# Expert sums in two half arrays, one bank for token and channel groups, and plain copies for five tiles

## The chip, the cores and the metric

The kernel runs on one core of a Trainium2 chip. The metric is the device time of one launch in microseconds; lower is better. PE is TensorE, DVE is VectorE, ACT is ScalarE, POOL is GpSimd, SP is SyncE with its DMA queue.

## The reference

The input x is (16, 64, 36, 100): batch, channel, height, width. The reference computes

```
y = x + sweeps(layernorm_over_channels(x))      # 9-tap convolutions with relu, row after row down and up, then column after column right and left
t = y as tokens (16*3600 tokens of 64 channels)
t = t + ffn(layernorm(t))
ffn(z): p = softmax(z @ router_w + router_b); the two largest of 8, rescaled to sum 1;
        sum over those two experts of p_e * (z @ expert_w[e] + expert_b[e])
```

The change touches only the last part, from the tokens on.

## The kernel before, in words

All of y stays in SBUF (`act_buf`), two image rows side by side: partitions 0 to 63 hold the channels of one row of a pair, partitions 64 to 127 those of the other. After the sweeps the token stage goes over the 18 row pairs. One row pair has 1600 columns (width times batch) in 13 tiles of 128, the last of which overlaps its neighbour and adds only 64 new columns (`TAIL`). The work of one row pair is called a region. Each region computes the experts of row pair j and, between them, prepares the tokens of row pair j + 1 (`now`). The last region prepares nothing. Buffers alternate by `slot`.

Preparation goes in 5 groups of up to three tiles (`TC`, `NCK`):

- `tokens` (PE, L974): y times a centring matrix with the router's columns behind it, 128 tokens by 144 columns, in PSUM bank `CT`, in two fp32 passes per tile.
- `copy_tokens` (ACT, L473 and L474): squares, and a copy to SBUF (`tl`).
- `square_sums` (DVE, L724), `inv_std_tokens` (ACT, L481 and L483): the inverse deviation.
- `scale_tokens` (POOL, L335 and L336): tokens and logits times the inverse deviation.
- `channels` (PE, L988): transposes back to channels, in bank `TB`.
- `first_part` (ACT, L491) and `second_part` (DVE, L732): high and low part of the normalised tokens, in fp32r.
- `softmax` (DVE, L748 to L764): 17 small steps for the whole row pair, with one exponential on ACT (L496), which give the gates of the two best experts and zero for the others.

The experts of a tile p:

- `experts` (PE, L1007): for each of the two image rows (q = 0, 1), 64 rows of the array, 512 columns (8 experts times 64 channels), three fp32r terms; q = 0 in the upper half of the array, q = 1 in the lower. The result is in one of two pairs of banks, `twin[0]` and `twin[1]`.
- `gate_tile` (DVE, L792): times the gates, into an SBUF buffer (`scratch`, `late` or `more`) of 8 experts by 128 columns. For tiles in `ACT_TILES` (6 to 12) DVE does only q = 0 and `gate_odd` (ACT, L506) does q = 1 with 8 instructions, one per expert, since the gate is then one scalar per partition.
- `pair_sums` (POOL, L322): experts 0 to 3 plus experts 4 to 7, 512 elements in place.
- `sum_experts` (PE, L1019): four full 128 x 128 transposes that accumulate in bank `SUM`, `LAG` = 2 tiles behind the experts. A gathering of four tiles (`QUAD`) fills the bank.
- `add_out` (DVE, L800): the bank plus y, into y.

SP stores a row pair when all its additions are done.

The order of each engine's instructions is written out by hand: a loop over the 13 tiles, with tables and fixed offsets that say beside which tile each piece of preparation stands. `STEP_AT` places the softmax steps. Engines meet through semaphores: `s_p` experts done, `s_g` and `s_ga` gated by DVE and ACT, `s_ps` pair sum done, `s_y` sum done, `s_o` addition done, `s_cp` token group copied, `s_xn2` group scaled, `s_tb`, `s_th` and `s_tl` channel group, its high part and its low part done. `experts` of tile p waits for the gating of tile p - 2. The first sum of a gathering waits for the addition of the gathering before.

```
for p in range(TILES):                    # the region on PE, before
    experts(j, slot, p)
    if now is not None:
        if 5 <= p < NCK + 5: channels(now, 1 - slot, p - 5)
        if p < NCK: tokens(now, 1 - slot, p)
    if p >= LAG: sum_experts(j, slot, p - LAG)
    elif later(j): sum_experts(j - 1, 1 - slot, TILES + p - LAG)
```

Of the kernel before, what the change touches and what calls it, by code (L numbers as in the profile page):

```python
# [7 lines left out]
ALU = mybir.AluOpType  # L8
# [4 lines left out]
def metaformer_kernel(nc, x, x_col, w_d, w_u, w_r, w_l, router_w, router_b, expert_w, expert_b, out):  # L13
# [24 lines left out]
    with ctx:  # L38
# [40 lines left out]
        gated = [scratch[:, 0:E * P], scratch[:, E * P:2 * E * P], late[:, 0:E * P], more[:, :]]  # L79
        gated = [g.rearrange("p (e m) -> p e m", e=E) for g in gated]  # L80
# [5 lines left out]
        sq = sb("sq", [P, 2, NC])  # L86
        lnv = sb("lnv", [P, 2, NC])
        rstd = sb("rstd", [P, 2, NC])
# [33 lines left out]
        def act_gates(j, p):  # L122

            return len(ACT_TILES) * j + sum(a <= p for a in ACT_TILES)
# [12 lines left out]
        def stage_age(slot, p):  # L137

            k = TILES * slot + p
            return next(d for d in range(1, SEQ) if stage_of(k - d) == stage_of(k))  # L140
# [5 lines left out]
        def later(n):  # L146
# [8 lines left out]
        STEP_AT = [(6, 2), (7, 0), (7, 1), (7, 2), (8, 0), (8, 1), (8, 2), (9, 0), (9, 2), (10, 0), (10, 1), (10, 2),  # L155
                   (11, 0), (11, 1), (11, 2), (12, 0), (12, 1)]
        EXP_TILE = STEP_AT[GAP_STEP - 1][0] + 1

# [106 lines left out]
        def _(pool):  # L265
# [51 lines left out]
            def pair_sums(j, slot, p):  # L317
                pool.wait_ge(s_g, TILES * j + p + 1)
                if p in ACT_TILES:
# [18 lines left out]
            def region(j, slot, now):  # L338
                for p in range(TILES):
                    if now is not None and 2 <= p < NCK + 2:  # L340
                        scale_tokens(now, 1 - slot, p - 2)
                    pair_sums(j, slot, p)
# [12 lines left out]
        def _(act):  # L355
# [109 lines left out]
            def copy_tokens(j, slot, c, bank=CT):  # L465
# [19 lines left out]
            def first_part(j, slot, c, bank=TB):  # L485
# [24 lines left out]
            def region(j, slot, now):  # L510

                for p in range(TILES):
                    if now is not None:
                        if p == EXP_TILE:
                            exponential(now)
                        if 5 <= p < NCK + 5:
                            first_part(now, 1 - slot, p - 5)
                        if p < NCK:
                            copy_tokens(now, 1 - slot, p)
                    if p in ACT_TILES:  # L520
                        gate_odd(j, slot, p)
                    if now is not None and 1 <= p < NCK + 1:
                        inv_std_tokens(now, 1 - slot, p - 1)
# [18 lines left out]
        def _(dve):  # L542
# [184 lines left out]
            def second_part(j, slot, c, bank=TB):  # L727
# [39 lines left out]
            def softmax(j, slot, at):  # L767

                steps = softmax_steps(j, slot)
                for k in range(SMN):  # L770
                    if STEP_AT[k] == at:
                        if k == 0:
                            dve.wait_ge(s_xn2, NCK * (j + 1))
                        elif k == EX_STEP:
                            dve.wait_ge(s_ex, j + 1)
                        if k > 0:
                            dve.wait_ge(s_sm, SMN * j + k)
                        steps[k]().then_inc(s_sm, 1)

            def gate_tile(j, slot, p):  # L780
# [7 lines left out]
                qs = 1 if p in ACT_TILES else 2  # L788
# [5 lines left out]
            def add_out(j, g):  # L794

                lo, hi = g * QUAD, min((g + 1) * QUAD, TILES)
                width, off = (QUAD * TN, 0) if hi < TILES else (TAIL, TN - TAIL)
                dst = flat(j)[:, lo * TN:lo * TN + width]
                dve.wait_ge(s_y, TILES * j + hi)
                nc.vector.tensor_tensor(dst, banks[SUM][:, off:off + width], dst, ALU.add).then_inc(s_o, 1)  # L800
# [10 lines left out]
            def region(j, slot, now):  # L811

                for p in range(TILES):
                    if now is not None and 1 <= p < NCK + 1:
                        square_sums(now, 1 - slot, p - 1)
                    gate_tile(j, slot, p)
                    if now is not None and 5 <= p < NCK + 5:
                        second_part(now, 1 - slot, p - 5)
                    for part in range(3):
                        if part == 2:  # L820
                            add_behind(j, p)
                        if now is not None:
                            softmax(now, 1 - slot, (p, part))
# [6 lines left out]
            for p in range(TILES):  # L830
                for part in range(3):
                    softmax(0, 0, (p, part))
# [12 lines left out]
        def _(pe):  # L845
# [120 lines left out]
            def tokens(j, slot, c, bank=CT):  # L966
# [11 lines left out]
            def channels(j, slot, c, bank=TB):  # L978
# [3 lines left out]
                if bank == TB:  # L982
                    if later(n):
                        pe.wait_ge(s_tl, n)
                elif c >= 2:
                    pe.wait_ge(s_tl, n - 1)
# [5 lines left out]
            def experts(j, slot, p):  # L992
# [6 lines left out]
                if p >= 2:  # L999
                    if p - 2 in ACT_TILES:  # L1000
                        pe.wait_ge(s_ga, act_gates(j, p - 2))
                elif later(j) and TILES + p - 2 in ACT_TILES:
# [8 lines left out]
            def sum_experts(j, slot, p):  # L1011
# [5 lines left out]
                at = (p % QUAD) * TN  # L1017
                for e in range(E // 2):
                    last = mm(banks[SUM][:, at:at + TN], stage(slot, p)[:, e], ident[:, :],  # L1019
                              start=e == 0, stop=e == E // 2 - 1, is_transpose=True)  # L1020
                last.then_inc(s_y, 1)

            def region(j, slot, now):
                for p in range(TILES):
                    experts(j, slot, p)
                    if now is not None:
                        if 5 <= p < NCK + 5:
                            channels(now, 1 - slot, p - 5)
                        if p < NCK:
                            tokens(now, 1 - slot, p)  # L1030
                    if p >= LAG:
                        sum_experts(j, slot, p - LAG)
                    elif later(j):
                        sum_experts(j - 1, 1 - slot, TILES + p - LAG)

# [82 lines left out]
```

## Time and profile before

| | |
|---|---|
| median of 3 runs | 1408.58 us (1408.44 to 1409.0) |
| the profiled execution's own time | 1407.74 us |
| span of the profiled execution | 1406.0 us |
| token stage: first gating, last addition begins | 936.51 us, 1401.78 us |
| one region with preparation | 25.97 us |

The span is the time between the first and the last recorded instruction of one execution; the rest of the run's time lies around it. Page shares are of the whole span. In the rows below, a group of instructions is named by its line in the kernel. A matmul's record is longer than its share of the array, since successive ones overlap. Durations of groups (xN) run from the first start to the last end.

### The profile page before, as it was taken

How to read it: one execution, taken by the hardware profiler on the slowest of the kernel's cores; microseconds unless marked ns; L12 is line 12 of the kernel's file. 1: busy time of each engine (PE TensorE's matmuls, PEld its weight loads, DVE VectorE, ACT ScalarE, POOL GpSimd, SP SyncE). 2: the span in 40 equal slices, each digit the busy share in tenths (PEclk: the TensorE clock that was granted, in tenths of full speed). 3: DMA queues.
4: the chain of work that ended last, by engine and by line, in shares of the span. 5: the costliest groups of instructions: out<-in, count | busy, mean ns of one | idle time of the engine just before them, and what ended most of it. 6: DMA issues, size and time to landing. Idle time of an engine off the chain costs nothing.

```text
span 1406.0 us, 30169 instructions
## 1 busy us (share of the span) xinstructions
PE 1345.1 (96%) x9344; PEld 1180.1 (84%) x9344; DVE 854.8 (61%) x1786; ACT 670.4 (48%) x2169; POOL 625.9 (45%) x752
## 2 busy tenths in 40 slices
PE   6899999999998999999999999979999999999997
PEld 5899999999998999999999999956666666666664
DVE  4788888755555222222222222269989989889896
ACT  5576777533434222222100000048778778778775
POOL 3566666100000000000144444457787887887886
PEclk9999999999999999999999999989999999999999
DMA  4112121100000000000011111100010100100101
GB/s 146 48 47 70 47 70 47 43 0 0 0 0 0 0 0 0 0 0 0 21 63 63 63 63 63 42 1 25 30 42 24 47 25 24 48 24 24 48 24 48
DMA packets 15372, 46.68 MB, mean 33 GB/s; under 512 B 2912, under 2 KB 2912, under 8 KB 15328
## 3 DMA queue, kind: packets, MB, share of 16 engines
q1 hardware_dynamic: 15184, 45.76, 9.3%
q8 instruction: 28, 0.46, 0.1%
q10 hardware_dynamic: 144, 0.33, 0.1%
q14 instruction: 16, 0.13, 0.0%
HBM read 31.33 MB, written 14.75 MB: 33 GB/s over the span
## 4 chain that ended last, share of the span: by engine, by line
PE 85%; DVE 6%; ACT 4%; issue 3%; POOL 1%; DMA 0%; DVEq 0%; POOLq 0%; ACTq 0%
PE twin L951 33%; PE twin L868 26%; PE twin L1007 9%; PE twin L1019 6%; PE twin L974 5%; PE twin L859 2%; PE twin L853 2%; PE twin L988 2%; ACT late L506 1%; DVE parts L732 1%; DVE scratch L792 1%; ACT more L506 1%; DVE act_buf L800 1%; ACT parts L491 1%; DVE twin L750 0%
## 5 line engine op out<-in xcount | busy, mean ns | idle before, releaser
L951 PE MATMUL twin<-kbuf,late 128*128 128x136 f32 (+2 forms) x3940 | 458.2, 280 | 5.0 <-DVE kbuf L700 5.0
L951 PEld LDWEIGHTS twin<-kbuf,late 128*128 128x128 f32 x3940 | 458.0, 192 | 5.3 <-DVE kbuf L700 5.3
L868 PE MATMUL twin<-parts 128*128 128x384 f32 (+2 forms) x2070 | 392.8, 341 | 0.0
L868 PEld LDWEIGHTS twin<-parts 128*128 128x128 f32 x2070 | 371.2, 188 | 2.8 <-issue 2.5
L297 POOL TENSOR_TENSOR act_buf<-kbuf,x_in 128x144 f32 (+1 forms) x198 | 96.6, 488 | 564.8 <-DVE kbuf L706 564.8
L706 DVE SCALAR_TENSOR_TENSOR kbuf<-twin,act_buf 128x144 f32<-128x144 f32 x394 | 121.3, 308 | 337.2 <-PE twin L951 337.2
L1007 PE MATMUL twin<-em,parts 64*128 64x512 f32 x1404 | 227.7, 429 | 5.0 <-DVE scratch L792 2.7
L322 POOL TENSOR_TENSOR scratch<-scratch 128x512 f32<-128x512 f32 x126 | 160.7, 1278 | 53.7 <-ACT scratch L506 36.7
L473 ACT ACTIVATE x_in<-twin 128x384 f32<-128x384 f32 (+1 forms) x90 | 40.3, 447 | 302.0 <-PE twin L974 302.0
L1007 PEld LDWEIGHTS twin<-em,parts 64*128 64x128 f32 x1404 | 116.7, 186 | 55.0 <-issue 36.7
L459 ACT ACTIVATE act_buf<-kbuf 128x144 f32 x196 | 63.2, 323 | 167.5 <-DVE kbuf L706 167.5
L792 DVE TENSOR_TENSOR scratch<-twin,scratch 128x512 f32<-128x512 f32 (+1 forms) x126 | 120.1, 953 | 17.3 <-PE twin L1007 13.1
L506 ACT ACTIVATE scratch<-twin,scratch 128x64 f32<-128x64 f32 x504 | 113.5, 415 | 0.8 <-PE twin L1007 0.4
L279 POOL TENSOR_TENSOR x_parts<-x_in,eps_c 128x400 fp32r<-128x400 f32 x66 | 56.3, 853 | 99.2 <-PE twin L853 81.0
L1019 PE MATMUL twin<-ident,scratch 128*128 128x128 f32 x504 | 78.4, 278 | 19.3 <-DVE act_buf L800 16.5
L281 POOL TENSOR_TENSOR x_parts<-x_in,x_parts 128x400 fp32r<-128x400 f32 x66 | 92.8, 1407 | 5.2
L322 POOL TENSOR_TENSOR late<-late 128x512 f32<-128x512 f32 x63 | 80.6, 1280 | 26.1 <-ACT late L506 19.0
L974 PEld LDWEIGHTS twin<-cl_w,act_buf 128*128 128x128 f32 x468 | 63.2, 193 | 34.2 <-ACT x_in L474 24.8
L1019 PEld LDWEIGHTS twin<-ident,scratch 128*128 128x128 f32 x504 | 56.4, 141 | 39.6 <-POOL scratch L322 34.3
L431 ACT ACTIVATE parts<-scratch 128x400 fp32r<-128x400 f32 x68 | 36.6, 538 | 106.7 <-DVE scratch L656 106.7
L974 PE MATMUL twin<-cl_w,act_buf 128*128 128x144 f32 x468 | 81.9, 309 | 2.1 <-POOL act_buf L314 2.0
L577 DVE TENSOR_TENSOR act_buf<-twin,rstd 64x400 f32 (+1 forms) x132 | 75.3, 570 | 1.9
(102 smaller groups left out, 1535.8 us busy)
## 6 DMA issues: line engine op xcount, KB each, us to landing
x_in<-x SPq DMA_DIRECT2D x36, 400.0 KB, 3.5
x_in<-x_col SPq DMA_DIRECT2D x20, 720.0 KB, 4.1
result<-act_buf SPq DMA_DIRECT2D x36, 400.0 KB, 2.8
scratch<-L_conv_w_d ACTq DMA_DIRECT2D x1, 320.0 KB, 4.7
scratch<-L_conv_w_u SPq DMA_DIRECT2D x1, 320.0 KB, 6.1
late<-L_conv_w_r SPq DMA_DIRECT2D x1, 320.0 KB, 6.4
late<-L_conv_w_l SPq DMA_DIRECT2D x1, 320.0 KB, 7.2
ew<-L_ffn_expert_w SPq DMA_DIRECT2D x2, 128.0 KB, 6.2
```

The lines of the kernel that those rows point to most:

```text
L281: nc.gpsimd.tensor_tensor(x_parts[:, b, 1], src, x_parts[:, b, 0].bitcast(F32), ALU.subtract).then_inc(s_xp, 1)
L297: nc.gpsimd.tensor_tensor(cols[:, :, g, w], kbuf[:, g], x_blk[:, slot, i, g], ALU.add).then_inc(s_cb[g], 1)
L322: nc.gpsimd.tensor_tensor(buf[:, 0:4], buf[:, 0:4], buf[:, 4:8], ALU.add).then_inc(s_ps, 1)
L506: last = act.activation(stage(slot, p)[:, e, C:P], twin[(TILES * slot + p) % 2][:, 1, e * C:(e + 1) * C], ACT.Copy, scale=gate[slot][:, 2 ...
L577: return nc.vector.tensor_tensor(rows[a * C:(a + 1) * C, 2 * j + q, g], centred[half], inv[half], ALU.mult)
L706: nc.vector.scalar_tensor_tensor(kbuf[:, g], banks[CONV[g]][:, 0:NH].rearrange("p (j b) -> p j b", j=HP), 0.0, cols[:, :, g, w], ALU.max, ...
L792: nc.vector.tensor_tensor(dst, src, scl, ALU.mult).then_inc(s_g, 1)
L868: last = mm(acc[:, lo:hi], vw[:, k, wpart, si], carry[:, cpart, g, lo + s * BG:hi + s * BG], start=first and si == 0, stop=final and si == ...
L951: last = mm(banks[CONV[g]][:, lo * BG:hi * BG], hw[:, k, si], kbuf[:, g, lo + s:hi + s].rearrange("p j b -> p (j b)"), start=si == 0, stop ...
L974: last = mm(banks[bank][:, CLW * i:CLW * (i + 1)], flat[:, tile_lo(p):tile_lo(p) + TN], cl_w[:, :], start=True, stop=True)
L1007: last = mm(twin[(TILES * slot + p) % 2][:, q, 0:E * C], tok[half, slot, l, span], em[half, b], start=k == 0, stop=k == len(TERMS) - 1)
L1019: last = mm(banks[SUM][:, at:at + TN], stage(slot, p)[:, e], ident[:, :], start=e == 0, stop=e == E // 2 - 1, is_transpose=True)
```

## The change

- Expert sums: each transpose is done as two half-array transposes, tokens 0 to 63 and 64 to 127 of the tile, each from its own 64 partitions, with 64 columns of the identity, into two banks (`SUMS`, 4 and 5). A bank holds 64 columns for each of eight tiles, so `QUAD` is 8, and two gatherings per region (8 and 5 tiles) take the place of four. An addition reads both banks in one instruction; the last gathering has one for four tiles and one for the tail.
- Token and channel groups share one bank (`CTB`, 7), so each group waits for the one before to be read out.
- `ACT_TILES` becomes (9, 11, 12). For `COPY_TILES` (0, 6, 7, 8, 10) ACT copies the q = 1 half without gates in one instruction of 512 elements, POOL multiplies that half by the gates in place of its addition, and PE sums all 8 experts instead of 4. Tile 0 is thus no longer gated whole by DVE.
- `LAG` is 3. There are six gated buffers instead of four; the two new ones lie on `sq`, `lnv` and `rstd`, which the token stage doesn't use. A buffer comes round after five tiles in most cases.
- Tables place every piece of the preparation. At one place PE does channels before tokens, ACT does the exponential, high parts, deviations, then copies, and DVE reductions, low parts, then softmax steps.

```diff
-        CT, TB = 4, 5
-        LOG, SUM = 6, 7
+        SUMS, LOG, CTB = [4, 5], 6, 7
-        FILL_CT, FILL_TB = [4, 0, 1, 2, 3], [5, 7, 5, 7, 5]
-        ACT_TILES = (6, 7, 8, 9, 10, 11, 12)
+        FILL_CT, FILL_TB = [7, 0, 1, 2, 3], [4, 5, 7, 4, 5]
+        ACT_TILES = (9, 11, 12)
+        COPY_TILES = (0, 6, 7, 8, 10)
-        LAG = 2
+        LAG = 3
-        QUAD = 4
+        QUAD = 8
-            return k % 4 if k < SEQ - 6 else (k - (SEQ - 6)) % 3
+            return k if k < 6 else (k - 6) % 5
-        STEP_AT = [(6, 2), (7, 0), (7, 1), (7, 2), (8, 0), (8, 1), (8, 2), (9, 0), (9, 2), (10, 0), (10, 1), (10, 2),
-                   (11, 0), (11, 1), (11, 2), (12, 0), (12, 1)]
+        TURN_AT = [(0, 0), (1, 1), (2, 1), (3, 1), (4, 1)]
+        COPY_AT = [(0, 0), (1, 0), (2, 1), (3, 1), (4, 1)]
+        VAR_AT = [(0, 0), (2, 0), (3, 0), (3, 2), (4, 2)]
+        INV_AT = [(2, 1), (3, 1), (4, 0), (5, 1), (6, 0)]
+        SCALE_AT = [(2, 0), (3, 0), (4, 0), (4, 0), (4, 0)]
+        BACK_AT = [(5, 1), (7, 0), (7, 1), (9, 0), (11, 0)]
+        HIGH_AT = [(6, 0), (6, 1), (8, 0), (8, 1), (10, 1)]
+        LOW_AT = [(5, 2), (7, 0), (7, 2), (9, 0), (11, 0)]
+        STEP_AT = [(6, 2), (7, 1), (7, 1), (8, 0), (8, 0), (8, 1), (9, 0), (10, 0), (10, 2), (11, 0), (11, 0), (11, 1), (11, 1), (12, 0), (12, 1), (12, 1), (12, 2)]
+        EXP_AT = (10, 1)
...
 pair_sums (POOL):
+                if p in COPY_TILES:
+                    odd = buf[:, :, C:P]
+                    scl = gate[slot][:, 2 * p + 1].unsqueeze(2).to_broadcast([P, E, C])
+                    nc.gpsimd.tensor_tensor(odd, odd, scl, ALU.mult).then_inc(s_ps, 1)
+                    return
                 nc.gpsimd.tensor_tensor(buf[:, 0:4], buf[:, 0:4], buf[:, 4:8], ALU.add).then_inc(s_ps, 1)
...
 gate_odd (ACT):
+                if p in COPY_TILES:
+                    src = twin[(TILES * slot + p) % 2][:, 1, :].rearrange("p (e c) -> p e c", e=E)
+                    act.activation(stage(slot, p)[:, :, C:P], src, ACT.Copy).then_inc(s_ga, 1)
+                    return
...
 add_out (DVE):
-                nc.vector.tensor_tensor(dst, banks[SUM][:, off:off + width], dst, ALU.add).then_inc(s_o, 1)
+                if hi < TILES:
+                    dst = flat(j)[:, lo * TN:hi * TN].rearrange("p (t r n) -> p r t n", r=2, n=C)
+                    src = twin[SUMS[0] // 2][:, :, 0:(hi - lo) * C].rearrange("p r (t n) -> p r t n", n=C)
+                    nc.vector.tensor_tensor(dst, src, dst, ALU.add).then_inc(s_o, 1)
...
 tokens (PE):
-                    if bank == CT:
+                    if c > 0 and bank == CTB:
                         pe.wait_ge(s_cp, n)
+                    elif c == 0:
+                        pe.wait_ge(s_tl, n)
...
 channels (PE), in a region:
+                elif c == 0:
+                    pe.wait_ge(s_cp, NCK * (j + 1))
+                else:
+                    pe.wait_ge(s_tl, n)
...
 sum_experts (PE):
-                at = (p % QUAD) * TN
-                for e in range(E // 2):
-                    last = mm(banks[SUM][:, at:at + TN], stage(slot, p)[:, e], ident[:, :],
-                              start=e == 0, stop=e == E // 2 - 1, is_transpose=True)
+                col, count = (p % QUAD) * C, E if p in COPY_TILES else E // 2
+                for e in range(count):
+                    for r in range(2):
+                        half = slice(r * C, (r + 1) * C)
+                        last = mm(banks[SUMS[r]][:, col:col + C], stage(slot, p)[half, e], ident[half, half],
+                                  start=e == 0, stop=e == count - 1, is_transpose=True)
                 last.then_inc(s_y, 1)
...
 the region on PE:
                 for p in range(TILES):
+                    for place in range(3):
+                        if place == 1:
+                            experts(j, slot, p)
+                        elif place == 2:
+                            if p >= LAG:
+                                sum_experts(j, slot, p - LAG)
+                            elif later(j):
+                                sum_experts(j - 1, 1 - slot, TILES + p - LAG)
+                        if now is not None:
+                            for c in at(BACK_AT, p, place):
+                                channels(now, 1 - slot, c)
+                            for c in at(TURN_AT, p, place):
+                                tokens(now, 1 - slot, c)
```

## Rows read from the trace of the kernel before

**Rows 1.** The page: busy us, share of the span and instructions of each engine.
```profile
PE 1345.1 (96%) x9344; PEld 1180.1 (84%) x9344; DVE 854.8 (61%) x1786; ACT 670.4 (48%) x2169; POOL 625.9 (45%) x752
```
**Rows 2.** Busy time by stretch, one region with preparation.
```profile
core 0: us, PE busy (x) PEld busy (x) DVE busy (x) ACT busy (x) POOL busy (x), PEclk, DMA share, GB/s
1113.25:1139.23 25.98, 24.61 (x169) 16.73 (x170) 23.42 (x45) 19.70 (x85) 21.00 (x24) 1.00 0.08 32
```
**Rows 3.** Timeline, PE: start, us, engine, line, operation, operands, count.
```profile
1110.48 0.30 PE L988 MATMUL twin<-ident,x_in 128*128 128x128 f32 x1 [0.16 <-DVE parts L732]
...
1113.25 0.63 PE L1019 MATMUL twin<-ident,scratch 128*128 128x128 f32 x4 [0.92 <-DVE act_buf L800]
1113.81 0.97 PE L1007 MATMUL twin<-em,parts 64*128 64x512 f32 x6
1114.70 0.66 PE L1019 MATMUL twin<-ident,scratch 128*128 128x128 f32 x4
1115.29 0.97 PE L1007 MATMUL twin<-em,parts 64*128 64x512 f32 x6
...
1119.93 1.00 PE L974 MATMUL twin<-cl_w,act_buf 128*128 128x144 f32 x6
...
1126.71 0.51 PE L974 MATMUL twin<-cl_w,act_buf 128*128 128x144 f32 x2
```
**Rows 4.** Timeline, PE, narrow window: two pairs of expert matmuls.
```profile
1113.81 0.73 PE L1007 MATMUL twin<-em,parts 64*128 64x512 f32 x4
```
**Rows 5.** Timeline, weight loads, narrow windows: two transpose loads, four expert loads.
```profile
1106.49 0.14 PEld L988 LDWEIGHTS twin<-ident,x_in 128*128 128x128 f32 x1 [0.37 <-POOL x_in L336]
...
1106.49 0.20 PEld L988 LDWEIGHTS twin<-ident,x_in 128*128 128x128 f32 x2 [0.37 <-POOL x_in L336]
...
1105.60 0.30 PEld L1007 LDWEIGHTS twin<-em,parts 64*128 64x128 f32 x4 [0.17 <-DVE late L792]
```
**Rows 6.** Timeline, DVE, in one region.
```profile
1110.65 0.37 DVE L753 TENSOR_TENSOR scratch<-rank_w,twin 128x208 f32<-128x208 f32 x1
1111.05 0.38 DVE L754 SCALAR_TENSOR_TENSOR twin<-scratch,twin 128x208 f32<-128x208 f32 x1
1111.34 0.68 DVE L792 TENSOR_TENSOR scratch<-twin,scratch 128x512 f32<-128x512 f32 x1
...
1118.14 1.23 DVE L792 TENSOR_TENSOR scratch<-twin,scratch 128x1024 f32<-128x1024 f32 x1 [0.30 <-DVE scratch L764]
1119.28 0.68 DVE L800 TENSOR_TENSOR act_buf<-twin,act_buf 128x512 f32 x1
1119.88 0.54 DVE L724 TENSOR_REDUCE stat<-x_in 128x6 f32<-128x384 f32 x1
1120.34 1.21 DVE L792 TENSOR_TENSOR late<-twin,scratch 128x1024 f32<-128x1024 f32 x1
```
**Rows 7.** Timeline, ACT, in one region.
```profile
1109.40 1.81 ACT L506 ACTIVATE scratch<-twin,scratch 128x64 f32<-128x64 f32 x8
1110.97 0.41 ACT L491 ACTIVATE parts<-twin 128x128 fp32r<-128x128 f32 x1
...
1118.86 0.49 ACT L473 ACTIVATE x_in<-twin 128x384 f32<-128x384 f32 x1 [0.67 <-PE twin L974]
```
**Rows 8.** Timeline, POOL, in one region.
```profile
1118.27 2.51 POOL L322 TENSOR_TENSOR scratch<-scratch 128x512 f32<-128x512 f32 x2 [0.35 <-ACT scratch L506]
...
1125.33 0.84 POOL L336 TENSOR_TENSOR x_in<-x_in,stat 128x384 f32<-128x384 f32 x1
...
1132.01 0.41 POOL L336 TENSOR_TENSOR x_in<-x_in,stat 128x128 f32<-128x128 f32 x1
```
**Rows 9.** PE's waits in one region: us in total, times, longest.
```profile
PE twin L1019 <- DVE act_buf L800: 0.9, 1, 0.9
```
**Rows 10.** Timeline, DVE: first gating and last addition of the last region.
```profile
1378.02 1.23 DVE L792 TENSOR_TENSOR scratch<-twin,scratch 128x1024 f32<-128x1024 f32 x1
...
1401.78 0.23 DVE L800 TENSOR_TENSOR act_buf<-twin,act_buf 128x64 f32<-128x64 f32 x1 [0.94 <-PE twin L1019]
```

More of the change, by code:

```diff
@@ L78, in metaformer_kernel @@
         sq_parts = parts[:, 2 * 2 * TOKS - 2 * 2 * NC:].rearrange("p (b l n) -> p b l n", b=2, l=2)
-        gated = [scratch[:, 0:E * P], scratch[:, E * P:2 * E * P], late[:, 0:E * P], more[:, :]]
-        gated = [g.rearrange("p (e m) -> p e m", e=E) for g in gated]
         early = act_buf[:, (HP - 8) * REG:(HP - 8) * REG + 3 * 4 * NC].rearrange("p (k b n) -> p k b n", k=3, b=4)
         kbuf = sb("kbuf", [P, G, HP, BG])
-        sq = sb("sq", [P, 2, NC])
-        lnv = sb("lnv", [P, 2, NC])
-        rstd = sb("rstd", [P, 2, NC])
+        spare = sb("spare", [P, 3 * 2 * NC])
+        sq, lnv, rstd = (spare[:, 2 * NC * k:2 * NC * (k + 1)].rearrange("p (b n) -> p b n", b=2) for k in range(3))
+        gated = [scratch[:, 0:E * P], scratch[:, E * P:2 * E * P], late[:, 0:E * P], more[:, :],
+                 spare[:, 0:E * P], spare[:, E * P:2 * E * P]]
+        gated = [g.rearrange("p (e m) -> p e m", e=E) for g in gated]
         ident = sb("ident", [P, P])
@@ L139, in stage_age @@
             k = TILES * slot + p
-            return next(d for d in range(1, SEQ) if stage_of(k - d) == stage_of(k))
+            return next(d for d in range(1, SEQ + 1) if stage_of(k - d) == stage_of(k))
         def tiles_of(c):
@@ L153, in metaformer_kernel, with at @@
         EX_STEP = 12
-        STEP_AT = [(6, 2), (7, 0), (7, 1), (7, 2), (8, 0), (8, 1), (8, 2), (9, 0), (9, 2), (10, 0), (10, 1), (10, 2),
-                   (11, 0), (11, 1), (11, 2), (12, 0), (12, 1)]
-        EXP_TILE = STEP_AT[GAP_STEP - 1][0] + 1
+        TURN_AT = [(0, 0), (1, 1), (2, 1), (3, 1), (4, 1)]
[8 more added lines that the diff above has]
+        EXP_AT = (10, 1)
+        def at(table, p, place):
+            return [c for c, when in enumerate(table) if when == (p, place)]
         s_wd = sem("s_wd")
@@ L339, in region @@
                 for p in range(TILES):
-                    if now is not None and 2 <= p < NCK + 2:
-                        scale_tokens(now, 1 - slot, p - 2)
-                    pair_sums(j, slot, p)
+                    for place in range(2):
+                        if place == 1:
+                            pair_sums(j, slot, p)
+                        if now is not None:
+                            for c in at(SCALE_AT, p, place):
+                                scale_tokens(now, 1 - slot, c)
             for c in range(NCK):
@@ L462, in _, with copy_tokens @@
                 copy_back(u, u)
-            def copy_tokens(j, slot, c, bank=CT):
+            def copy_tokens(j, slot, c, bank=CTB):
                 n, b, k = NCK * j + c, (slot + c) % 2, len(tiles_of(c))
@@ L512, in region @@
                 for p in range(TILES):
[L513 to L523, printed above, removed]
+                    for place in range(2):
+                        if place == 1 and p in ACT_TILES + COPY_TILES:
+                            gate_odd(j, slot, p)
+                        if now is not None:
+                            if EXP_AT == (p, place):
+                                exponential(now)
+                            for c in at(HIGH_AT, p, place):
+                                first_part(now, 1 - slot, c)
+                            for c in at(INV_AT, p, place):
+                                inv_std_tokens(now, 1 - slot, c)
+                            for c in at(COPY_AT, p, place):
+                                copy_tokens(now, 1 - slot, c)
             for c in range(NCK + 2):
@@ L765, in softmax_steps, with softmax @@
                 ]
[L767 to L778, printed above, removed]
+            def softmax(j, slot, k):
+                if k == 0:
+                    dve.wait_ge(s_xn2, NCK * (j + 1))
+                elif k == EX_STEP:
+                    dve.wait_ge(s_ex, j + 1)
+                if k > 0:
+                    dve.wait_ge(s_sm, SMN * j + k)
+                softmax_steps(j, slot)[k]().then_inc(s_sm, 1)
             def gate_tile(j, slot, p):
@@ L813, in region @@
                 for p in range(TILES):
[L814 to L820, printed above, removed]
+                    for place in range(3):
+                        if place == 1:
+                            gate_tile(j, slot, p)
+                        elif place == 2:
                             add_behind(j, p)
                         if now is not None:
-                            softmax(now, 1 - slot, (p, part))
+                            for c in at(VAR_AT, p, place):
+                                square_sums(now, 1 - slot, c)
+                            for c in at(LOW_AT, p, place):
+                                second_part(now, 1 - slot, c)
+                            for k in at(STEP_AT, p, place):
+                                softmax(now, 1 - slot, k)
             for c in range(NCK + 2):
@@ L829, in _ @@
                     second_part(0, 0, c - 2, FILL_TB[c - 2])
-            for p in range(TILES):
-                for part in range(3):
-                    softmax(0, 0, (p, part))
+            for k in range(SMN):
+                softmax(0, 0, k)
             region(0, 0, 1)
@@ L976, in tokens, with channels @@
                 last.then_inc(s_ct, 1)
-            def channels(j, slot, c, bank=TB):
+            def channels(j, slot, c, bank=CTB):
                 n = NCK * j + c
                 pe.wait_ge(s_xn2, n + 1)
[L982 to L986, printed above, removed]
+                if not later(j):
+                    if c >= 3:
+                        pe.wait_ge(s_tl, c - 2)
+                elif c == 0:
+                    pe.wait_ge(s_cp, NCK * (j + 1))
+                else:
+                    pe.wait_ge(s_tl, n)
                 for i, p in enumerate(tiles_of(c)):
@@ L1024, in region @@
                 for p in range(TILES):
[L1025 to L1034, printed above, removed]
+                    for place in range(3):
+                        if place == 1:
+                            experts(j, slot, p)
+                        elif place == 2:
+                            if p >= LAG:
+                                sum_experts(j, slot, p - LAG)
+                            elif later(j):
+                                sum_experts(j - 1, 1 - slot, TILES + p - LAG)
+                        if now is not None:
+                            for c in at(BACK_AT, p, place):
+                                channels(now, 1 - slot, c)
+                            for c in at(TURN_AT, p, place):
+                                tokens(now, 1 - slot, c)
             pe.wait_ge(s_em, 9)
```

24 lines of the change are left out of this document (14 added, 10 removed).

## The prediction

> **What bounds the kernel now.** I read the page's shares first: TensorE is 96% busy, VectorE 61% [rows 1]. The change touches only the last third of the span, the token stage, from 936.5 us on (the table), so the next view is busy time by stretch there [rows 2]. One region (13 tiles of one row pair) repeats every 25.98 us, its neighbours within 0.02: PE 24.6 busy, DVE 23.4, POOL 21.0, ACT 19.7, clock 1.00, the upper of the two levels (2.4 GHz). 18 regions from 936.5 to 1378 and 1402 us are a third of the time; 17 of them carry the preparation of the next region, the last does not [rows 10]. "Busy" flatters PE, since pipelined records overlap, so I price PE by starts [rows 3]. Where nothing is awaited, experts begin at 1113.81, sums at 1114.70, experts at 1115.29: 0.89 + 0.59 = 1.48 us for a tile.
>
> Inside that: three pairs of expert matmuls (upper and lower half array together). Four records last 0.73, six 0.97 [rows 3, 4], so a pair that follows a pair adds 0.235 us, and three in a flow cost 0.705. A sum transpose adds 0.11 us (one lasts 0.30, four 0.63), four 0.44. That makes 1.14; the missing 0.33 to 0.34 us is the change between half-array and full-array work and back, in which the array runs empty and the first weights are not preloaded.
>
> PE's region: experts 13 x 0.705 = 9.17; sums 52 x 0.109 = 5.67; channel transposes 13 x 0.109 = 1.42; token matmuls 26 x 0.1225 = 3.19 (six last 1.00, two 0.51, so 0.49 for four); 13 round trips x 0.33 = 4.29. Sum 23.7, so only 2.2 us of the 25.98 are waits; the longest, 0.9, is on the L800 addition [rows 9].
>
> **PE after the change.** (a) Expert sums. A full transpose (128 moving columns) becomes two half-array ones with 64 columns each, into different banks. What does such a pair cost? The rows say that moving columns set the pace: 0.1225 us for 144 columns and 0.109 for 128 are both 0.85 ns per column, so 64 columns are 0.055 us. The load must not be slower: after an idle stretch two transpose loads of 0.14 us each fill 0.20 us together, so the second began 0.06 after the first [rows 5]. And two half-array loads do run side by side: four expert loads of 0.18 fill 0.30, two and two [rows 5]. I take 0.057 us per pair, as nearest; it has not been seen for this form, and the bounds are 0.055 and 0.22 (four issues of 0.055, the densest spacing that the rows show: a load and a transpose in 0.109). Eight tiles have 4 pairs, the five copy tiles 8 (POOL no longer adds their two halves of experts): 72 pairs x 0.057 = 4.1 us instead of 5.67.
> By "LDWEIGHTS (loading the stationary operand)" in the Trainium skill's page "TensorE: Matmul & The Clock Gate", 128 weight columns would take about 107 ns however few rows they have; by that rule the sums would be 72 x 0.107 = 7.7 us, not 4.1. The expert loads fit it (second pair of loads 0.1 after the first), the transpose loads, 0.06 apart, do not.
> (b) Sums now have the experts' array shape, so the round trip remains only at the 5 token and 5 channel groups: 10 x 0.33 = 3.3 instead of 4.29.
> PE's region: 9.17 + 4.1 + 1.42 + 3.19 + 3.3 = 21.2 us, 2.5 less.
>
> **DVE.** Prices from start to next start [rows 6]: gating of a whole tile 1.14, of half a tile 0.60, reduction 0.46 and a low part of the same size as much (0.20 for the one-tile group), addition 0.60 per 512 elements (the tail 0.15), a softmax step 0.41 before a dependent one, 0.29 otherwise. Half a tile is as long as the 512-element addition. Whole tiles fall from 6 to 5, half tiles rise from 7 to 8: -0.54. Additions: 3 x 0.60 + 0.15 become 1.14 (1024 elements, priced as the 1024-element gating) + 0.60 + 0.15: -0.06. Walking the new tables gives 10.5 gating + 4.1 reductions and low parts + 1.9 additions + 5.5 softmax = 22.0 us. DVE becomes the longest engine.
>
> **ACT.** A gated odd half is 8 instructions, 1.57 us (1109.40 to 1110.97) [rows 7]. Seven such become three, plus five plain copies of 512 elements: one of 384 is 0.49 long, 0.39 of it until the next can start, so 0.50 for 512. 11.0 becomes 4.7 + 2.5; 3.8 us go. ACT ends near 16 us and is cover for everything moved on its queue.
>
> **POOL.** It issues the same number of operations. Five additions (1.25 each, two in 2.51) become scalings of 512 elements by a broadcast. L336, the same kind, has 384 in 0.84 and 128 in 0.41, hence 512 in 1.05; bounds 1.05 and 1.28 [rows 8]. 8 x 1.25 + 5 x 1.05 + token scaling 4.8 = 20.0 us. Below DVE, so it costs nothing unless it comes late: three token scalings now stand together ahead of tile 4's addition.
>
> **One bank for tokens and channels; lag 3; moved tables.** All ten groups pass one bank, so each waits for the one before it to be read out. In the channel groups: transposes 0.65, ACT high part 0.5, DVE low part 0.5, then the next may start. I walked one region on paper with the prices above. In tiles 0 to 4 PE has 10.0 us against DVE's 8.0, but starts some 2 us ahead; DVE loses 0.4 in waits for experts. Groups 0 to 2 of the channels (tiles 5 to 8) come late through the bank: DVE waits 0.1, 0.55 and 0.2 and the refill between them. POOL holds tile 4's sum until 12.1 us after the region's start, and its transposes stand at 12.9, so no wait. The eighth-tile sum waits for the addition at tile 10 (PE idle 0.8, hidden since DVE is the bound). Second addition 0.15. In all 1.5 us on DVE: period 22.0 + 1.5 = 23.5. The longer lag (three tiles instead of two, buffers six instead of four) is free: every buffer's last sum is issued before its next expert matmul. No DMA is added or moved; SP waits for fewer, coarser additions, which only the last store could feel.
>
> **Last region.** From its first gating (1378.0) to its last addition (1402.0) it takes 24.0 us [rows 10], paced by ACT's seven tiles. After: POOL 8 x 1.25 + 5 x 1.05 = 15.3, first gating 0.65, ACT's tiles 11 and 12 late by about 0.7, last sum and two additions 1.3: 18.0. Gain 6.0. The fill before 936.5 is a chain of scaling, transposes and softmax that the bank table does not shorten: 0.
>
> **Sum.** 17 x (25.98 - 23.5) = 42.2, plus 6.0: 48.2 us. The profiled execution took 1407.74 (span 1406.0 and 1.74 around it), 0.84 below the median of 1408.58. 1359.5 for the former is 1360.4 against the median.
>
> **Rivals.**
> 1. *Gain eaten on PE.* Either the load rule above holds (pair 0.107), or the round trips stay because it is the data type (fp32r experts, fp32 transposes) that empties the array and not its shape: 13 x 0.33 = 4.3 more. No row here separates the two, since no half-array fp32 transpose exists. Against the second: under "Key Properties" in the Trainium skill's "TensorEngine Tiling (Array Packing)" it is the change of tiling mode that drains, so it would vanish. PE is then 24.8 to 25.5, plus about 1 of waits: 25.6 to 26.4 per region. 17 x (-0.4 to +0.4) and -6: 1396 to 1409. Chance 0.2.
> 2. *Slower: PE's issue.* A copy tile now wants 32 PE instructions in 0.46 us, 14 ns apiece; the densest sustained spacing in the rows is 0.055. If small half-array pairs are issued at that pace, or the halves don't overlap and also empty the array between them, a pair costs up to 0.22: 72 x 0.163 = 11.7 more, PE 32.9, period about 34: 1408.6 + 17 x 8 = 1545. It decides from about 0.13 per pair on (PE 26.5), where 17 x 0.5 outweighs the last region's 6. For it: doubled instruction count. Against it: load pairs and matmul pairs of the experts start together. Chance 0.13.
> 3. *POOL or the bank chain is worse than walked* (copies at 1.28, another 0.3 per channel group): period 24.6, 1379. This is inside my forecast's own range.
> Forecast, chance 0.67, own range 1345 (period 22.6, waits of 0.6) to 1380.
>
> **Range and chances.** 0.2% (2.8 us) is about what a measurement of this kernel tells from no change. The forecast's own range holds some 0.57; reaching 8 in 10 takes in most of rival 1: 1343 to 1406. Faster: 0.67 + 0.10 of rival 1 = 0.77; within: 0.09; slower: 0.14.
>
> **What would show it.** PE rows: sums with 64 x 128 weights, four pairs adding 0.23 us, eight adding 0.46; experts' six records in 0.86 rather than 0.97 next to them. Stretches: about 23.5 us a period, DVE about 22.5 busy, ACT about 16. Waits: DVE on ACT's L491 and on PE channels. Wrong if eight pairs take 0.85 or more, if experts still take 0.97 everywhere, or if POOL's tile operations end the waits.

## The result and the profile after

The changed kernel takes 1358.74 us (median of 4 runs, 1357.32 to 1360.26) against 1408.79 us: a ratio of 0.9641, 95% interval 0.9624 to 0.9658. The forecast was 1360.4 us and faster.

The page's busy line and the stretch of one region after, in the columns of [rows 1, 2]:

```profile
PE 1306.0 (96%) x11000; PEld 1181.9 (87%) x11000; DVE 831.0 (61%) x1768; ACT 609.6 (45%) x1683; POOL 603.4 (44%) x752
```
```profile
1104.11:1127.34 23.23, 22.32 (x263) 16.61 (x262) 22.27 (x44) 16.31 (x55) 20.09 (x24) 1.00 0.09 37
```

A region takes 23.23 us instead of 25.98 (forecast 23.5). The shares of the whole span hardly moved; the stretch shows what did. ACT fell by 3.4 us, PE by 2.3, DVE by 1.15, POOL by 0.9. PE and DVE are now about equally full.

The last region, DVE's timeline; these rows answer to [rows 10]:

```profile
1333.49 0.69 DVE L815 TENSOR_TENSOR late<-twin,scratch 128x512 f32<-128x512 f32 x1
...
1353.81 0.21 DVE L830 TENSOR_TENSOR act_buf<-twin,act_buf 128x64 f32<-128x64 f32 x1
```

Where the 48.0 us between the two spans (1406.0 and 1358.0) went: 17 regions from the first gating to that of the last region took 441.5 us and take 395.5 (-46.0); the last region took 24.0 and takes 20.5 (-3.5). The first gating came 1.5 us later, at 938.0. The row sweeps, which the change leaves alone, took 1.4 us longer in this execution, the slowest of the four (granted clock 0.92 in its first 25 us, 1.00 before); in eleven of the twelve variants below the first gating stands at 935.4 to 936.5.

PE's timeline in one region of the changed kernel, to be read against [rows 3, 4]:

```profile
1113.29 0.52 PE L1023 MATMUL twin<-ident,x_in 128*128 128x128 f32 x3 [0.37 <-DVE parts L758]
1113.74 0.47 PE L1056 MATMUL twin<-ident,scratch 64*128 64x64 f32 x8
1114.01 0.94 PE L1042 MATMUL twin<-em,parts 64*128 64x512 f32 x6
1114.79 0.41 PE L1056 MATMUL twin<-ident,late 64*128 64x64 f32 x8
...
1116.41 0.66 PE L1056 MATMUL twin<-ident,more 64*128 64x64 f32 x16
1116.87 0.94 PE L1042 MATMUL twin<-em,parts 64*128 64x512 f32 x6
1117.65 0.65 PE L1056 MATMUL twin<-ident,spare 64*128 64x64 f32 x16
...
1119.99 0.71 PE L1056 MATMUL twin<-ident,scratch 64*128 64x64 f32 x16 [0.52 <-DVE act_buf L824]
...
1121.26 0.43 PE L1056 MATMUL twin<-ident,scratch 64*128 64x64 f32 x8
1121.63 1.00 PE L1007 MATMUL twin<-cl_w,act_buf 128*128 128x144 f32 x6
```

Where they follow experts at once, sixteen half transposes last 0.65 to 0.66 and eight 0.41: four pairs more cost 0.24 to 0.25, a pair 0.06. From experts to sums it is now 0.78 us (1116.87 to 1117.65), not 0.89, and from eight pairs to the next experts 0.46 (1116.41 to 1116.87). Between sums and experts most of the old cost is gone, but experts still take more than three pairs in a flow (0.705).

POOL and ACT, timelines, the two operations that are new:

```profile
1114.27 1.04 POOL L338 TENSOR_TENSOR more<-more,scratch 128x512 f32<-128x512 f32 x1
```
```profile
1111.28 0.60 ACT L528 ACTIVATE more<-twin 128x512 f32<-128x512 f32 x1 [0.23 <-PE twin L1042]
```

Both prices are as forecast: 1.05 on POOL, and 0.60 on ACT, of which about 0.1 overlaps what follows at once. The gathered addition of 1024 elements (L824) is 1.22 us long and 1.13 to the next start, against 1.14 priced.

### The profile page after: what moved, and what is told of

Read it like the earlier page. It is cut to its first block, busy times and chain, and to the rows that moved or that the text cites. A ratio compares the mean times of both kernels' runs of the same rounds, so it can differ in the third digit from the quotient of the medians.

```text
span 1358.0 us, 33006 instructions
## 1 busy us (share of the span) xinstructions
PE 1306.0 (96%) x11000; PEld 1181.9 (87%) x11000; DVE 831.0 (61%) x1768; ACT 609.6 (45%) x1683; POOL 603.4 (44%) x752
## 4 chain that ended last, share of the span: by engine, by line
PE 85%; DVE 7%; issue 4%; ACT 2%; POOL 0%; DMA 0%; DVEq 0%; POOLq 0%; ACTq 0%
PE twin L982 34%; PE twin L899 27%; PE twin L1042 8%; PE twin L1007 5%; PE twin L1056 5%; PE twin L890 2%; PE twin L884 2%; PE twin L1023 2%; DVE act_buf L824 1%; DVE scratch L815 1%; ACT parts L512 1%; DVE late L815 1%; PE twin L921 0%; DVE twin L775 0%; DVE scratch L777 0%
## 5 line engine op out<-in xcount | busy, mean ns | idle before, releaser
L1042 PE MATMUL twin<-em,parts 64*128 64x512 f32 x1404 | 224.5, 423 | 3.4 <-DVE scratch L815 2.3
L340 POOL TENSOR_TENSOR scratch<-scratch 128x512 f32<-128x512 f32 x54 | 69.2, 1281 | 22.0 <-ACT scratch L531 11.4
L603 DVE TENSOR_TENSOR act_buf<-twin,spare 64x400 f32 (+1 forms) x132 | 75.3, 570 | 1.9
L815 DVE TENSOR_TENSOR scratch<-twin,scratch 128x512 f32<-128x512 f32 (+1 forms) x90 | 75.0, 842 | 2.1 <-PE twin L1042 1.4
L354 POOL TENSOR_TENSOR x_in<-x_in,stat 128x384 f32<-128x384 f32 (+1 forms) x90 | 67.0, 745 | 0.0
L389 ACT ACTIVATE spare<-twin,eps_c 128x400 f32<-128x400 f32 x66 | 39.3, 595 | 61.2 <-PE twin L890 61.2
L685 DVE TENSOR_TENSOR parts<-scratch,parts 128x400 fp32r<-128x400 f32 x68 | 39.2, 576 | 41.1 <-ACT parts L452 41.1
L682 DVE SCALAR_TENSOR_TENSOR scratch<-twin,act_buf 128x400 f32<-128x400 f32 x68 | 39.1, 575 | 36.9 <-PE twin L899 36.4
```

The costliest lines, as they stand in the source:

```text
L354: nc.gpsimd.tensor_tensor(xn, xn, inv.to_broadcast([P, k, 2, C]), ALU.mult).then_inc(s_xn2, 1)
L603: return nc.vector.tensor_tensor(rows[a * C:(a + 1) * C, 2 * j + q, g], centred[half], inv[half], ALU.mult)
L815: nc.vector.tensor_tensor(dst, src, scl, ALU.mult).then_inc(s_g, 1)
L1042: last = mm(twin[(TILES * slot + p) % 2][:, q, 0:E * C], tok[half, slot, l, span], em[half, b], start=k == 0, stop=k == len(TERMS) - 1)
```

## The experiments

All ratios are to the kernel before, runs of the same chip and job. "Period" is the median spacing of regions in the run's profile. In the diffs, `...` stands for lines left out.

### The two halves of the change, together and apart

The parts form a square: sums by half or full transposes, five copies or none, inside the changed frame (tables, shared bank, lag, gathering of eight).

**full_sums** (the additions read the two banks in the matching order)

```diff
...
-                col, count = (p % QUAD) * C, E if p in COPY_TILES else E // 2
+                col, count = (p % 4) * TN, E if p in COPY_TILES else E // 2
                 for e in range(count):
-                    for r in range(2):
-                        half = slice(r * C, (r + 1) * C)
-                        last = mm(banks[SUMS[r]][:, col:col + C], stage(slot, p)[half, e], ident[half, half],
-                                  start=e == 0, stop=e == count - 1, is_transpose=True)
+                    last = mm(banks[SUMS[p % QUAD // 4]][:, col:col + TN], stage(slot, p)[:, e], ident[:, :],
+                              start=e == 0, stop=e == count - 1, is_transpose=True)
```

> The changed kernel, but each sum transpose is a full 128 x 128 one again (4 per gated tile, 8 per copy tile), still eight tiles to a gathering. Theory A (PE's cheap half-array pairs and the missing array changes carry the gain): sums 72 x 0.109 = 7.9 us instead of 4.2, 13 round trips instead of 10, so about 4.7 us more PE per region, PE 25.9, period 26.3 to 27, time 1410 to 1422. Rival B (the gain comes from the relief of ACT and DVE and from the new tables): time stays below 1375.

Measured: 1430.42 us, ratio 1.0151 (1.0134 to 1.0168), period 27.20. Theory A's direction, 8 us beyond its range; rival B falls. The stretch:

```profile
1138.46:1165.66 27.20, 26.31 (x192) 18.77 (x190) 22.69 (x45) 16.46 (x55) 19.93 (x24) 1.00 0.08 31
```

Half-array sums are worth 4.0 us per region when the copies are there, 72 us in all.

**no_copies**

```diff
-        ACT_TILES = (9, 11, 12)
-        COPY_TILES = (0, 6, 7, 8, 10)
+        ACT_TILES = (6, 7, 8, 9, 10, 11, 12)
+        COPY_TILES = ()
```

> The changed kernel with no copy tile: tiles 6 to 12 gated by ACT expert by expert, tile 0 whole by DVE, tables as changed. Theory A with waits: PE falls by 20 pairs (1.2 us), DVE rises by 0.54, but ACT rises by 3.8 to 20 us and, since experts of tile p wait for the gating of p - 2, tiles 6 to 12 go at ACT's 1.6 us or more: period 24 to 24.8, time 1372 to 1386. Rival (half-array sums alone do it): at or below 1362.

Measured: 1397.68 us, ratio 0.9916 (0.99 to 0.9933), period 25.28. The half sums do not do it alone, but it is 12 us above theory A's range. These views say why; waits of one region first (engine, line, releaser; us in total, times, longest):

```profile
DVE parts L758 <- ACT parts L512: 2.4, 4, 1.0
...
PE twin L1023 <- DVE parts L758: 1.6, 1, 1.6
```

In the changed kernel the first of these is 0.3. The chain of waits ahead of PE's wait:

```profile
1127.21 1.14 ACT more L531 x5
1128.35 0.39 ACT parts L512
1128.76 0.57 DVE parts L758
```

A channel group's high part (L512) stands behind a gated tile of eight ACT instructions, DVE waits for it, and PE for DVE. Then PE's timeline and the stretch behind that wait (last columns: clock, DMA):

```profile
1129.46 0.52 PE L1023 MATMUL twin<-ident,x_in 128*128 128x128 f32 x3 [1.60 <-DVE parts L758]
...
1130.19 1.50 PE L1042 MATMUL twin<-em,parts 64*128 64x512 f32 x6
...
1132.87 1.36 PE L1042 MATMUL twin<-em,parts 64*128 64x512 f32 x6
```
```profile
1129.40:1134.30 4.90, 4.83 (x44) 3.66 (x44) 3.68 (x9) 3.49 (x16) 3.78 (x4) 0.65 0.00 0
```

After PE's thinner stretch (busy 1.84 of the 3.00 us from 1126 to 1129) the granted clock was at the lower of its two levels (1.2 GHz) for a part of the next ones, mean 0.65, and six expert matmuls took 1.50 and 1.36 us instead of 0.94. Six regions of this run have such a stretch; counted from one first softmax step (L774) to the next, they are 25.5 to 26.2 long. The others are 24.8 to 25.5, the lower figure being the one that theory A had as its upper end; the rest of the spread is the loop turn shown under pe_light. The 17 regions took 431.3 us, 9.4 more than at 24.8 each; the six stretches are about 6 of that. The changed kernel holds 1.00 in its stretch. The wait alone does not decide it: PE waits 1.2 to 1.6 us for L758 in each of the 17 regions, and after twelve of these waits the clock stayed at 1.00, as here:

```profile
1180.47 0.52 PE L1023 MATMUL twin<-ident,x_in 128*128 128x128 f32 x3 [1.58 <-DVE parts L758]
...
1181.19 0.94 PE L1042 MATMUL twin<-em,parts 64*128 64x512 f32 x6
```

What else it takes is open.

**frame_only** is both edits at once: neither half sums nor copies.

> The changed kernel with full 128 x 128 sums and without copy tiles: what is left of the change is the shared bank, the lag of three, six buffers, the gathering of eight and the tables. Theory A (PE is the bound with full sums): PE 23.7 us of work as before plus the waits of the shared bank and of ACT's seven tiles: period 26.0 to 27.0, time 1407 to 1424; the frame alone gives nothing. Rival (the tables carry part of the gain): below 1400.

Measured: 1411.27 us, ratio 1.001 (1.0001 to 1.0019), period 26.16. The frame alone gives nothing, as theory A said.

**before_copies** puts the five copies (ACT's plain copy, POOL's scaling, eight full transposes) into the kernel before, with its own tables, bank, lag and gathering.

> The kernel before with the copy tiles alone (full transposes, old tables, old lag). Theory A: PE was at its limit, five tiles have 4 more transposes each (20 x 0.109 = 2.2 us), part hidden in the 2.2 us of waits that ACT's relief removes: period 26.2 to 27, last region shorter, time 1408 to 1424. Rival B (relief of ACT is itself a gain): below 1400.

Measured: 1430.98 us, ratio 1.0151 (1.0131 to 1.0171), period 27.31: 7 us above theory A's range, and rival B falls here too.

| period, us | no copies | five copies |
|---|---|---|
| kernel before, full sums | 25.98 | 27.31 |
| changed frame, full sums | 26.16 | 27.20 |
| changed frame, half-array sums | 25.28 (24.8 to 25.5 at full clock) | 23.23 |

The copies lose 1.0 to 1.3 us under full sums and win 2.05 under half-array sums. Each half is a doubtful trade alone: copies take some 3.4 us off ACT and put 20 full transposes (2.2 us) on PE, which had no room; half sums make room on PE, but then ACT's tiles set the pace. Which parts of the frame (shared bank, lag, buffers, tables) the pair of halves needs was not tried one by one. Half sums as written here use a second sum bank, and the old frame has none free.

### Which engine binds now

**dve_light** (the eight-tile addition for the first of its eight tiles only):

```diff
-                    nc.vector.tensor_tensor(dst, src, dst, ALU.add).then_inc(s_o, 1)
+                    nc.vector.tensor_tensor(dst[:, :, 0:1], src[:, :, 0:1], dst[:, :, 0:1], ALU.add).then_inc(s_o, 1)
```

> The changed kernel, the addition of eight gathered tiles done for one column of each only (the other 1008 of 1024 elements of it are left out of the output), so DVE has 1.0 us less per region. Theory A (DVE is the bound now): 0.6 to 1.0 of it comes back, 17 or 18 times: 1340 to 1349. Rival (PE or the shared bank is the bound): within 4 us of 1359.

Measured: 1345.3 us, ratio 0.9549 (0.9533 to 0.9565), period 22.50. The edit does a little less than was expected of it: the third index counts tiles, so one whole tile is added, 128 of 1024 elements, in 0.28 us instead of 1.22. 0.73 of the 0.94 came back.

**pe_light** (copy tiles summed over four experts: `count` is always E // 2):

> The changed kernel, copy tiles summed over 4 of the 8 experts only (the other four experts of tiles 0, 6, 7, 8, 10 are left out of the output): 20 pairs of half-array transposes less, 1.2 us of PE per region. Theory A (DVE is the bound, PE has slack): at most 0.4 us of it comes back per region, 1352 to 1360. Rival (PE is still the bound): 1.0 or more per region, 1342 or less.

Measured: 1348.22 us, ratio 0.9562 (0.9547 to 0.9578), median period 22.51. Between the two: about half of the 1.2 us over all 17 regions (mean 22.68). That DVE alone is the bound falls here.

The mean is above the median because two kinds of region alternate. DVE's timeline from the last softmax step to the next region's first reduction, twice:

```profile
1072.82 0.37 DVE L790 TENSOR_TENSOR scratch<-twin,best 128x208 f32<-128x208 f32 x1
1073.12 0.54 DVE L750 TENSOR_REDUCE stat<-x_in 128x6 f32<-128x384 f32 x1
...
1095.32 0.37 DVE L790 TENSOR_TENSOR scratch<-twin,best 128x208 f32<-128x208 f32 x1
1095.91 0.55 DVE L750 TENSOR_REDUCE stat<-x_in 128x6 f32<-128x384 f32 x1 [0.21 <-issue]
```

The second time DVE starts 0.3 us later and waits for nothing that the profile shows. This happens six times, in every second region. The region loop does two regions per pass and turns six times, at just these places, so I take it for the cost of the loop's turn on DVE. From one L824 to the next, pe_light's regions with a turn are 22.8 to 23.1 long, the others 22.5. The changed kernel has the same six delays, yet its regions are 23.21 to 23.28 with or without one: there a DVE that is 0.3 late at the region's start costs nothing, and with less work on PE it costs all of it.

**pool_light** (POOL adds three pairs of experts instead of four: `buf[:, 0:3]` and `buf[:, 4:7]`):

> The changed kernel, POOL adds three pairs of experts instead of four in the eight tiles that are not copied (one pair is left out of the output): about 0.3 us less for each of these additions, 2.4 us of POOL per region. Theory A (POOL is cover): 0.2 us per region at most, 1355 to 1360. Rival (POOL, late after its three scalings in a row, sets the sums): 0.5 us per region or more, 1350 or less.

Measured: 1357.52 us, ratio 0.9627 (0.9612 to 0.9642), period 23.23, as in the changed kernel. POOL's additions are cover.

The chain of waits through one region of the changed kernel (start, us, what) shows how both can bind:

```profile
1108.87 0.75 PE twin L1042 x6
1109.62 0.48 PE twin L1023 x3
1110.10 0.39 PE twin L1056 x8
1110.49 0.75 PE twin L1042 x6
...
1112.06 0.50 ACT parts L512
1112.58 0.05 DVE parts L758
...
1116.87 0.37 DVE twin L780
...
1118.63 1.23 DVE act_buf L824
1119.85 0.14 issue
1119.99 0.71 PE twin L1056 x16
1120.70 0.75 PE twin L1042 x6
```

It runs on PE until tile 6, passes through the channel group's high part to DVE, stays there until the addition at tile 10, and goes back to PE at tile 11, where the sum of tile 8, the first of the next gathering, waits for that addition. Theory C is this chain: PE from tile 11 to 6, DVE from 7 to 10.

**copy_1** adds tile 1 to the copy tiles.

> The changed kernel with tile 1 as a sixth copy tile (nothing left out). DVE 0.54 us less per region, PE four pairs more (0.24), ACT one copy more (0.5), POOL 0.2 less. Theory A (DVE is the bound): 0.2 to 0.5 us per region come back, 1350 to 1356. Rival (in the first tiles, PE sets the pace, and DVE only waits longer there): 1358 to 1364.

Measured: 1363.79 us, ratio 0.9671 (0.9657 to 0.9684), period 23.49. It lost 0.25 us per region, the price of four pairs, and the 0.54 that DVE gained were worth nothing there: in tiles 0 to 4 PE binds.

**both_light** is pe_light and dve_light in one.

> The two lightened kernels in one: copy tiles summed over 4 experts (PE) and the addition of eight tiles done for one column each (DVE); both parts of the output are left out. Theory C (the region's chain runs on PE in tiles 11 to 6 and on DVE in tiles 7 to 10, one after the other): the two savings add up, 0.74 + 0.58 to 0.72 per region, period 21.8 to 21.9, time 1333 to 1338. Theory A (DVE alone is the bound): no more than the DVE part, 1343 or more. Rival (PE and DVE are parallel bounds that hide each other): clearly more than the sum, below 1329.

Measured: 1340.67 us, ratio 0.9504 (0.9489 to 0.9518), period 22.24. Theory A's limit (1343) and theory C's range (1333 to 1338) both fail: 0.99 us per region came where each alone gave 0.7. Its chain shows what stands close behind:

```profile
1100.32 0.84 POOL x_in L354
1101.16 0.23 POOL scratch L353
1101.39 0.80 POOL x_in L354
...
1107.54 1.54 ACT scratch L531 x7
...
1110.44 0.85 ACT more L531 x4
```

POOL's token scalings ahead of the first channel group and ACT's gated tiles 9, 11 and 12 take DVE's place. So theory C holds as far as the first 0.7 us, and a third chain ends it. That chain is read from this one trace; no run makes ACT or POOL lighter on top.

**whole_0** (`COPY_TILES = (6, 7, 8, 10)`, tile 0 whole on DVE), **copy_5_for_0** (`(5, 6, 7, 8, 10)`) and **copy_4_for_0** (`(4, 6, 7, 8, 10)`) tried to use theory C.

> The changed kernel, tile 0 gated whole by DVE again, not copied (nothing left out). PE loses four pairs (0.24) at tile 3, DVE gets 0.54 more at tile 0, ACT and POOL little. Theory C: PE is the bound in both places, so 0.1 to 0.24 us per region are won: 1354 to 1358. Theory A (DVE is the bound): up to 0.54 per region lost: 1362 to 1369.

> The changed kernel with tile 5 copied instead of tile 0 (nothing left out; the count of copies, transposes and gatings is the same). The four extra pairs move from tile 3, where PE is the bound, to tile 8, where DVE is; DVE's 0.54 move from tile 5 to tile 0. Theory C: 0.2 to 0.6 us per region won, 1348 to 1355. Theory A (only totals count): 1357 to 1361.

> The changed kernel with tile 4 copied instead of tile 0 (nothing left out). The four extra pairs move from tile 3 to tile 7, at the seam of the two stretches; DVE's 0.54 move from tile 4 to tile 0. Theory C: 0.1 to 0.4 us per region won, 1350 to 1357. Theory A (only totals count): 1357 to 1361.

Measured: 1359.39 us, 0.9638 (0.9625 to 0.9651); 1363.83 us, 0.9671 (0.9658 to 0.9684); 1362.49 us, 0.9657 (0.9643 to 0.967). All three miss: the first equals the changed kernel, the others lose (17 regions took 400.5 and 398.4 us instead of 395.5). The chain of copy_5_for_0 has a piece that the changed kernel's has not:

```profile
1109.29 1.28 POOL scratch L340
1110.57 0.23 POOL scratch L353
1110.80 0.54 POOL x_in L354
```

Here POOL's addition and the three scalings behind it are on the chain up to the first softmax step (L774). The chains of whole_0 and copy_4_for_0 have this piece too. DVE's waits in whole_0, from 940 to 1340 us:

```profile
DVE scratch L774 <- POOL x_in L354: 8.4, 16, 0.6
```

copy_4_for_0 has the same, copy_5_for_0 4.2 us in 17 waits; the changed kernel has 0.2 us, once. The loop's turns show what this path does. In whole_0 the regions without a turn are 23.12 long, 0.1 under the changed kernel's, as theory C said; those with one are 23.45 to 23.77, and the two cancel. So in whole_0 a late DVE is on the path at the region's start, through POOL. All three kernels have in common that tile 0 is gated whole by DVE; that this is what brings POOL onto the chain fits, but no run makes POOL lighter in them. No variant beats the changed kernel.

## Why the prediction was right, and its steps that were not

**Right.** The price of a half-array pair decided it: 0.057 forecast, 0.06 measured. That the moving columns set it, as I assumed from the rate of 0.85 ns per column, is not shown: 64 columns come to 0.055, the two loads of [rows 5] are 0.06 apart, and the measured price fits either. The rule of 107 ns for 128 weight columns, in "LDWEIGHTS (loading the stationary operand)" of the Trainium skill's "TensorE: Matmul & The Clock Gate", does not hold for these loads: pairs of 128 columns follow each other every 0.06 us.

Most of the cost of the change went with the shape, not with the data type: transposes in another data type but the same shape follow the experts after 0.78 us instead of 0.89, and experts follow eight of them after 0.27 (1113.74 to 1114.01), while token matmuls of the transposes' own type but another shape follow after 0.37 (1121.26 to 1121.63). So the first rival fell; with it the drain on a change of tiling mode ("Key Properties" in "TensorEngine Tiling (Array Packing)" of the Trainium skill) agrees with the trace. The second rival, PE's issue, fell too: 32 instructions of a copy tile pass in 0.46 us.

The first rival's price for the data type was too high, though. Before, 13 round trips cost 4.3 us; if the type made them, there would still be 13 in all, and 10 were already in my 21.2. So 1.0 us was to be added and not 4.3, which gives PE 22.2, close to what it turned out to be for another reason, and a period within the forecast's own range. In that form the total could not have told rival and forecast apart; the rows above do.

**Mis-sized: the experts after a sum.** I took three pairs in a flow, 0.705 us, as if the first pair cost no more than the others. It is 0.78, so about 13 x 0.075 = 1.0 us more PE work per region than 21.2; the stretch of 23.23 us less PE's waits of 0.5 and 0.4 gives 22.3. The six records last 0.94 next to sums, where I wrote 0.86. Why the first pair costs more is open: data type and kind of work change there together.

**Failed: "DVE becomes the longest engine", and everything else is cover.** By totals it was near (22.27 busy, PE 22.32), and I read the period as DVE's total plus its waits. pe_light shows that PE's work counted just as much: the chain is on PE in nine of thirteen tiles. PE's wait for the addition, which I called hidden, is a link of it. The period came out 0.27 under mine: DVE idled 0.96 instead of 1.5; the high parts cost it 0.34 where I had 0.85 in three waits. A little too much waiting stood against a little too little work, so 23.5 was also luck.

**Mis-sized: the last region.** 18.0 us forecast, 20.5 measured. I let POOL set its pace and ACT come late by 0.7. In its chain three gated tiles stand in series with the experts:

```profile
1344.48 1.75 ACT scratch L531 x8
...
1346.37 0.98 PE twin L1042 x6
...
1347.45 1.75 ACT more L531 x8
1349.22 0.05 issue
1349.26 0.52 ACT spare L531 x2
```

Experts 11 wait for the gating of tile 9, so 1.75 + 0.98 us come one after the other. That rule was in my own account of the kernel, and I did not apply it to this region.

**The sum.** 17 x 2.71 (the mean) = 46.0 where 42.2 was forecast, and 3.5 where 6.0: 49.5 against 48.2. The two errors nearly cancel. The medians are 50.05 us apart. **The fill** was priced at 0; from the last column step to the first gating it is 0.3 shorter (20.66 against 20.99). The copies' worth (39 us, part of it clock) stood in no step of its own: I had called ACT "cover" and so would have forecast almost nothing for the copies by themselves.

## What to carry to other kernels

Price a transpose or a small matmul by the records of its own kind: how two rates scale with columns, and how far apart two loads start after an idle stretch. Two trades that each lose or hardly win alone can be worth 50 us together when one makes the room that the other fills, so read the limits after both changes, not after each. Where two engines are about equally full, walk the chain through the period: a change pays only in the stretch where its engine binds, and the next chain may be close behind, here 0.3 us after the first 0.7. A delay that comes in some regions only, like a loop's turn, is a free experiment: see whether the regions that have it are longer.

## What was not expected of the hardware

- The experts' first pair costs more even without a change of array shape: 0.78 us from experts to the next operation after sums, against 3 x 0.235 = 0.705.
- A wait of 1.6 us on PE within a thinly busy stretch (1.84 of 3.00 us) was followed by the lower clock level in five regions of no_copies and not in the other twelve, where the wait was 1.2 to 1.6 us. Where it came, a region took up to 1 us more. The changed kernel's waits in its stretch, 0.52 us at the longest, left the clock at 1.00.
- At each of the six places where the region loop turns, DVE starts its next instruction 0.3 us later than elsewhere, with no wait in the profile. The changed kernel hides it; pe_light and whole_0 pay 0.35 us.
